# Attention kernel on one core: the value products of a step in two halves of 256 query columns, between the tiles of the maximum pass

## The reference

```python
x = x + tanh(g_xattn) * xattn(layernorm(x), ctx, ctx)
x = x + tanh(g_ffn) * ffn(layernorm(x), wg, W, b)

# xattn(q, k, v): 16 batches of 8 heads with 16 features, 512 queries, 512 keys
qk = einsum('bdm,bdn->bmn', qh, kh) / sqrt(16)
ret = einsum('bmn,bcn->bcm', softmax(qk, axis=-1), vh)

# ffn: one of 8 experts for each of the 2048 rows of 512
probs = softmax(xt @ wg); idx = argmax(probs); gate = probs[idx]
out = gate * (xt @ W[idx].T + b[idx])
```

## Time and profile before

| | us |
|---|---|
| median of 3 runs | 651.05 (650.95 to 651.89) |
| the profiled execution | 653.81 |
| its span, first to last instruction | 652.2 |
| TensorE matmuls busy | 542.4 (83%) |
| VectorE busy | 448.6 (69%) |
| GpSimd busy | 370.7 (57%) |
| ScalarE busy | 350.3 (54%) |

### The profile page before, as it was taken

How to read it: one execution, slowest core, us unless ns; L and a number is a source line. 1 busy time by engine, 2 the same in 40 slices (tenths; PEclk the granted TensorE clock), 3 DMA queues, 4 the chain that set the end, 5 groups by cost and what they waited for, 6 DMA issues and landing times. The chain is left out here.

```text
span 652.2 us, 9589 instructions
## 1 busy us (share of the span) xinstructions
PE 542.4 (83%) x2603; PEld 183.4 (28%) x2603; DVE 448.6 (69%) x883; ACT 350.3 (54%) x429; POOL 370.7 (57%) x631
## 2 busy tenths in 40 slices
PE   0177989898999989899998989897869699389993
PEld 0011222232323223232322323232212155145551
DVE  5486788888888888888997878888956634101110
ACT  2112777677777767877776676865537621011110
POOL 5442648858585765858577575864542634424441
PEclk9999999999999999999999989999979879879997
DMA  4754375666667567664465665373410235233310
GB/s 144 178 156 147 76 179 152 176 169 177 186 160 215 152 179 171 167 190 109 141 165 105 164 115 167 75 143 78 95 53 2 87 124 163 73 116 114 118 65 0
DMA packets 35045, 85.52 MB, mean 131 GB/s; under 512 B 10232, under 2 KB 10364, under 8 KB 34976
## 3 DMA queue, kind: packets, MB, share of 16 engines
q1 hardware_dynamic: 22848, 59.46, 37.0%
q0 software_dynamic: 12160, 25.62, 12.1%
HBM read 62.56 MB, written 27.15 MB: 138 GB/s over the span
## 5 line engine op out<-in xcount | busy, mean ns | idle before, releaser
L801 DVE TENSOR_REDUCE neg_max<-ps_ring 128x1 f32<-128x512 f32 x512 | 332.0, 681 | 67.3 <-PE ps_ring L1129 62.9
L726 ACT ACTIVATE probs<-ps_scores 128x1024 f32<-128x1024 f32 x256 | 251.5, 1023 | 103.0 <-PE ps_scores L1147 98.4
L1129 PE MATMUL ps_ring<-stacks 96*128 96x512 bf16 x512 | 200.9, 406 | 58.8 <-DMA stacks<-parts_dram 30.0
L1147 PE MATMUL ps_scores<-stacks 128*128 128x512 bf16 x512 | 156.7, 389 | 19.5 <-DMA stacks<-shift_parts 11.1
L1166 PE MATMUL ps_pv<-probs,v_ones 128*32 128x512 f32 x1024 | 141.1, 624 | 0.0
L1129 PEld LDWEIGHTS ps_ring<-stacks 96*128 96x128 bf16 x512 | 49.5, 97 | 256.2 <-DVE neg_max L801 206.3
L1223 PE MATMUL ps_scores<-w_sb,f_xt 128*128 x184 | 85.2, 607 | 0.0
L1147 PEld LDWEIGHTS ps_scores<-stacks 128*128 128x128 bf16 x512 | 47.9, 102 | 64.9 <-ACT probs L726 17.8
L519 POOL DMA_DIRECT2D stacks<-shift_parts x96 | 50.0, 523 | 20.3 <-POOL shift_parts L512 18.0
L719 ACT COPY f_xt<-ps_scores 128x512 f32<-128x512 f32 x23 | 13.4, 586 | 86.4 <-PE ps_scores L1206 86.4
L444 POOL TENSOR_SCALAR rs<-mv 128x1 f32<-128x1 f32 x32 | 6.0, 187 | 90.6 <-DVE mv L817 45.3
(11 more groups left out here) (139 smaller groups left out, 479.1 us busy)
## 6 DMA issues: line engine op xcount, KB each, us to landing
parts_dram<-prep POOLq DMA_DIRECT2D x16, 768.0 KB
stacks<-parts_dram SPq DMA_DIRECT2D x64, 192.0 KB
stacks<-parts_dram SPq DMA_DIRECT2D x64, 128.0 KB
w_sb<-w_t SPq DMA_DIRECT2D x16, 512.0 KB, 8.6
recs_dram<-rec SPq DMA_DIRECT2D x16, 512.0 KB, 11.8
prep<-x_perm SPq DMA_DIRECT2D x16, 256.0 KB, 5.0
prep<-k_perm SPq DMA_DIRECT2D x16, 256.0 KB, 8.8
v_in<-v_t SPq DMA_DIRECT2D x16, 256.0 KB
```

The source lines that it names most:

```text
L726: nc.scalar.activation(probs[:, k % 2, 2 * jp:2 * jp + 2], ps_scores[:, jp], ACT.Exp).then_inc(exp_done, 1)
L801: nc.vector.tensor_reduce(neg_max[:, g, j, c:c + 1], ps_ring[:, u.slot(n)], AX.X, ALU.max, negate=True).then_inc(ring_free, 1)
L1129: nc.tensor.matmul(ps_ring[:, u.slot(n + c)], q_stack[0:KS, B.p, g, j, c * 128:(c + 1) * 128], k_stack[0:KS, B.p, g, j], start=True, stop= ...
L1147: last = nc.tensor.matmul(ps_scores[:, jp, j % 2], k_stack[0:KA, B.p, g, j, c * 128:(c + 1) * 128], q_stack[0:KA, B.p, g, j], start=True, ...
```

## The change

`values` gets a third argument, the half. For the first key block of a bank (c = 0) nothing is cut: half 0 does all 512 query columns, half 1 nothing. For c = 1 to 3 half 0 does columns 0 to 255 and half 1 columns 256 to 511; half 0 alone waits for the exponentials, half 1 counts `pv_done`. The order of a step becomes S0, R0, (T), V half 0, R1, S1, R2, V half 1, (turn_rows), R3, (route). So half 0, and all of V(0) and V(4), now stand ahead of R1 and S1. VectorE's and ScalarE's lists stay as they were.

```diff
-            def values(B, k):
+            def values(B, k, half):
 
                 g, c = divmod(k, NC)
-                pe.wait_ge(exp_done, B.b * (2 * STEPS) + (2 * k + 2))
+                if c == 0 and half == 1:
+                    return
+                cols = slice(0, DM) if c == 0 else slice(half * (DM // 2), (half + 1) * (DM // 2))
+                if half == 0:
+                    pe.wait_ge(exp_done, B.b * (2 * STEPS) + (2 * k + 2))
...
                 for j in range(NJ):
-                    last = nc.tensor.matmul(ps_pv[32 * j:32 * j + 32, g], v_ones[:, B.p, c, g, j], probs[:, k % 2, j],
-                                            start=c == 0, stop=c == NC - 1)
-                last.then_inc(pv_done, 1)
+                    last = nc.tensor.matmul(ps_pv[32 * j:32 * j + 32, g, cols], v_ones[:, B.p, c, g, j],
+                                            probs[:, k % 2, j, cols], start=c == 0, stop=c == NC - 1 and half == 1)
+                if c == 0 or half == 1:
+                    last.then_inc(pv_done, 1)
...
+                    attended = (B, k - 1) if k > 0 else (B.plus(-1), STEPS - 1)
+                    if k > 0 or prev:
+                        values(*attended, 0)
+                    if nxt:
+                        scores_for_max(B.plus(1), u, n - 1, k, (1,))
+                        n += 1
                     scores(B, k, 1)
                     if nxt:
-                        scores_for_max(B.plus(1), u, n - 1, k, (1, 2))
-                        n += 2
-                    if k > 0:
-                        values(B, k - 1)
-                    elif prev:
-                        values(B.plus(-1), STEPS - 1)
+                        scores_for_max(B.plus(1), u, n - 2, k, (2,))
+                        n += 1
+                    if k > 0 or prev:
+                        values(*attended, 1)
```

More of the change, by code:

```diff
@@ L1280, in _ @@
             route(last.plus(-1))
-            values(last, STEPS - 1)
+            values(last, STEPS - 1, 0)
+            values(last, STEPS - 1, 1)
             pe.wait_ge(w_loaded, 16 * NB)
```

## The result

| | before | changed |
|---|---|---|
| median | 651.82 us (648.10 to 657.06, 20 runs) | 659.52 us (655.06 to 665.33, 20 runs) |
| span of the profiled execution | 652.2 | 659.4 |
| mean granted clock | 0.962 | 0.968 |

The account below looks back on a forecast made before the run. A closed loop through GpSimd was taken to set ordinary batches, TensorE and VectorE only steps 5 to 0. Terms 2.0 (11 batches) - 0.3 (batches 0 and 1) + 0.3 + 1.1 = +3.1 us: median 654.2 us, range 647 to 664.

Parts of the forecast that it names:

- The closed loop through GpSimd sets the batch: Ordinary batches, 28.22 us: GpSimd's chain from mean1's start (m) fixes step 4's exponentials at m+12.80; only steps 5 to 0 count.
- The half block costs 0.57 and a split step 0.24 more: TensorE's value blocks: a half takes 0.57 us, a split step 3.07 instead of 2.83, by 0.24 fixed cost per block.
- the faster one: Rival: GpSimd's loop does not hold, steps 1 to 4 shrink too, 639 us; chance 0.13.
- The drain in full: Rival: TensorE drains 0.16 us per tiling switch, some 0.4 per split step instead of 0.24, 658 to 659 us; chance 0.12.
- The new wait is 1.04 and VectorE starves 1.3 to 1.4: Step 1: V(0) waits 1.04 us for the copied logits; VectorE idles 1.3 to 1.4 us before a maximum, formerly 0.43.
- GpSimd's chain is not delayed, and the stall is free: Step 1: V(0)'s 1.04 us stall costs the batch nothing, since GpSimd still gets its inputs in time.
- by 0.8 and 0.6: Slack in us: high half read by m+5.0, needed m+5.82; ScalarE done about m+10.5, first rest ready m+11.1.
- Step 5 loses 0.15, steps 6 and 7 gain 0.14, step 0 loses 0.17: Ordinary batch: V(4) delays R3, split steps shorten to 3.07 us, step 0 delays mean1; sum +0.18 us a batch.
- m+12.8 grows: Sign of error: step 4's exponentials start later than 12.8 us after mean1's start, so one margin was too narrow.
- The clock falls at the stall: Rival: TensorE's clock falls behind V(0)'s wait, +4 us for a third of 11 batches, +12 for all; 658 to 666; chance 0.18.
- Batches 13 and 14 pay 0.3, once: Without stats1 and mean1 ahead of the logits the stall is 0.3 us, added once since batch 14 waits for transfers.
- Batch 15 pays 1.1: No ring tiles there: V(0) and half of V(1) come between exponential and scores, 0.7, plus 0.4 for another half: +1.1 us.

Follow-up runs that it names:

- e5: The kernel before with GpSimd's split maxima ahead of the rstd for which it idles: 643.58 us, ratio 0.9867 to the kernel before.
- e8: The kernel before with one 128x512 copy more on GpSimd, behind the split maxima: 657.46 us, ratio 1.0088 to the kernel before.
- e9: The kernel before with the values cut in halves, side by side behind R2, nothing moved: 645.89 us, ratio 0.9977 to the kernel before.
- e1: The changed kernel with V(0) put back behind R2 of step 1: 649.81 us, ratio 1.0030 to the kernel before.
- e6: The changed kernel with GpSimd's split maxima ahead of the rstd: 654.70 us, ratio 1.0032 to the kernel before.
- e10: The changed kernel with V(0) behind R2 of step 1 in batches 12, 13 and 14 alone: 653.89 us, ratio 1.0108 to the kernel before.
- e12: The kernel before, whole value blocks, with V(0) alone moved behind R0 of step 1: 661.97 us, ratio 1.0193 to the kernel before.
- e7: The changed kernel with V(0) and V(4) behind R2 and GpSimd's split maxima ahead of the rstd: 646.48 us, ratio 0.9912 to the kernel before.
- e3: The changed kernel with both halves behind R2, R1 still ahead of S1: 660.38 us, ratio 1.0208 to the kernel before.
- e4: The changed kernel without the cut, the whole block behind R0 or T in every step: 684.11 us, ratio 1.0548 to the kernel before.
- e11: e5 with the halves and the changed order in steps 6 and 7 alone: 639.64 us, ratio 0.9865 to the kernel before.
- e2: The changed kernel with V(0) and V(4) put back behind R2 of steps 1 and 5: 649.64 us, ratio 1.0024 to the kernel before.

## Why the prediction was half right

- *The closed loop through GpSimd sets the batch:* right. Exponentials at m+12.80, GpSimd's idle 5.36, e5 and e8 move the batch from GpSimd alone.
- *The half block costs 0.57 and a split step 0.24 more:* right in size (0.57; steps 5 to 6 are 3.08 from R3 to R3, forecast 3.07), and e9 places it: it belongs to the switch.
- *The other rivals:* the faster one fell with its condition (the loop holds). The drain in full, 0.4 a split step, fell with the 3.08. The rule behind it in the Trainium skill (TensorEngine Tiling (Array Packing), Key Properties: changing the mode drains TensorE) agrees with e9 in kind, since the price sits at the changes between tiles and strips; the rows make it 0.24 for both.
- *The new wait is 1.04 and VectorE starves 1.3 to 1.4:* right, 1.05 and 1.41.
- *"GpSimd's chain is not delayed, and the stall is free", by 0.8 and 0.6; "batches 2 to 12 have this shape":* right for the ordinary batch (e1's batches are as long), wrong for batch 9. The two margins named hold (high half read at m+5.0); `turn_back` was not on the list, and it had no margin at all (e6). With the routing's operations on VectorE in batch 9 it came 1.5 us later than in e1, GpSimd's chain was delayed by 1.1, and the batch is 1.4 longer. "Wrong if m+12.8 grows" was met there: m+13.67.
- *Step 5 loses 0.15, steps 6 and 7 gain 0.14, step 0 loses 0.17:* from R3 of step 5 on, 3.08, 3.57 and 4.83 us against 3.15, 3.63 and 4.64: gains of 0.07 and 0.06, a loss of 0.19. R3 of step 5 comes 0.23 later instead of 0.15. Together +0.29 in this batch, +0.26 on the mean of both lengths, against +0.18: 2.8 us in 11 batches instead of 2.0.
- *The clock falls at the stall:* this was the rival with 0.18, priced for a third of the batches or all. It does fall in some batches, once in the changed kernel's profiled execution and in 4 of 23 over all with that wait, and a fall costs 1.2 to 1.6 us; the forecast's sum had no term for it. But the kernel before has falls of its own (two up to batch 13 in its profiled execution), and the mean clocks leave room for about one more a launch on average. The prediction looked for "the point from which it decides"; no such point came out of these runs.
- *Batches 13 and 14 pay 0.3, once:* wrong. The wait is 0.95 with nothing else ahead on VectorE, because the logits stand behind the maximum of the ring tile in front of V(0), a term that the 0.3 left out; VectorE starves 1.41 behind it in both batches, with no GpSimd loop to take it up. The two profiled executions differ by 2.8 from batch 12 on, of which 1.1 in batch 12 comes in e1 as well; e10 leaves open how much of it is the wait's.
- *Batch 15 pays 1.1:* 0.8.

The mis-sized terms all hang on the one edit that the prediction had called free, V(0) ahead of R1 and S1. e1 shows that directly: 5 of the 7 us go when V(0) stands where it stood. Of these 5, 1.7 are in batches 8 and 9 and come again in e6 and e10, which have the same order there; the clock and batches 12 to 14 share the rest, and how isn't settled. That 659.5 us still lies inside the stated range, 647 to 664, is luck in part: the range was that wide for the price of the halves and for a clock that falls in most batches, not for batches 9, 13 and 14.

## What to carry to other kernels

A stall that the critical chain covers is free only in the batches that have that chain, and only while nothing else is made faster or put into the same lists; list everything that stands behind the stalled instruction on every engine, down to the last one that another engine needs, and look at one batch of every kind, not at one ordinary batch. A stall on TensorE of about a microsecond can have a second price, since the clock fell behind it in some batches and not in others: count it over many stretches and several executions, of the kernel before as well, and set it against the mean clock of all executions. And where one engine idles in front of the list that sets the period, reordering that list (e5: -1.3%) is worth more than refining the engine that the busy shares point to.

## What the runs showed of the hardware

Four float32 matmuls in strips of 32 partitions with 256 columns, twice in a row, take the 1.00 us of four with 512. The halves cost more only with another kind of matmul between them.

VectorE's cast to int32 of 128x8 elements took 0.23 us in the changed kernel (at 337.22) and 2.87 in e5, where GpSimd's pair of `lows` started 0.55 behind it:

```profile
324.61 2.87 DVE L907 CAST dest_i<-dest_f 128x8 int32<-128x8 f32 x1
```
```profile
325.16 2.27 POOL L478 TENSOR_TENSOR prep<-prep 128x512 bf16<-128x512 f32 x2
```

It ended 0.05 us behind the pair's end, in e12 0.04 behind (342.78 and 2.77 us, the pair at 343.24). TensorE then waited 2.74 us for a bank in e5, and that batch lasts 33.20 us, where e7's batch 9 lasts 29.27. The cast took 2.7 to 2.9 us in e3, e4 and e11 too and some 0.2 in before, the changed kernel, e1, e2, e6, e7, e8, e9 and e10. One number parts the two groups: the pair starts 0.44 to 0.59 us behind the start of the cast in the five long ones and 0.73 to 1.13 behind it in the nine short ones (0.73 in the changed kernel).

The Trainium skill (SBUF — State Buffer, SBUF: two separate sides) says that some VectorE operations and GpSimd's exclude each other at a shared port for a whole instruction, and that the one that starts first goes first. The ends of the records agree with such a lock; but the cast's record starts first, and the cast waited for two instructions. Why it lost isn't shown. Any change of pace can move the two onto each other or apart, and one such meeting costs its batch some 4 to 8 us (e5 against e7, e12 against its batch 10 of 29.80 us). In the profiled executions of the pair before and after it plays no part; whether it came in others of the changed kernel's 20 the record can't tell.
